# The end of the up-sampling: GpSimd makes the even columns, VectorE derives the odd ones and rectifies within its addition

## What is computed

```python
out = bilinear_resize(x, 64, 64)
out = relu(bn(conv1x1(out, conv1_w), bn1_s, bn1_b))
out = att(out, ...)             # softmax attention over N = 4096 pixels, gamma * attention + out
out = relu(bn(out, bn2_s, bn2_b))
out = bn(conv1x1(out, conv2_w), bn3_s, bn3_b)
out = bilinear_resize(out, 128, 128)
return relu(out + shortcut)     # shortcut = x
```

## Time and profile before

| | |
|---|---|
| median of 3 runs | 2825.43 us (2825.24 to 2825.67) |
| span of the profiled execution, first to last instruction | 2825.0 us |
| busy: TensorE / VectorE / ScalarE / GpSimd | 87% / 91% / 55% / 66% |
| mean granted TensorE clock | 0.960 of full speed |

### The profile page before, as it was taken

How to read it: one execution, slowest core, us unless ns; L and a number is a source line. 1 busy time by engine, 2 the same in 40 slices (tenths; PEclk the granted TensorE clock), 3 DMA queues, 4 the chain that set the end, 5 groups by cost and what they waited for, 6 DMA issues and landing times.

```text
span 2825.0 us, 53992 instructions
## 1 busy us (share of the span) xinstructions
PE 2443.9 (87%) x15912; PEld 1698.8 (60%) x15912; DVE 2561.7 (91%) x3344; ACT 1548.0 (55%) x2753; POOL 1861.1 (66%) x1536
## 2 busy tenths in 40 slices
PE   2499998898899898888889898889989999999981
PEld 1267766666566666666646666656664766666660
DVE  9978789999879999999987999999997899999989
ACT  1146655555545565555655555555654666666662
POOL 7672078888727888888833888888891255554576
PEclk8799999999999999999999999999999999999995
DMA  5321012222202222222210222222220111111123
GB/s 171 97 58 40 1 45 89 82 90 75 83 16 74 77 90 90 82 75 90 83 47 31 83 90 75 90 83 78 87 94 4 46 68 64 63 60 60 60 83 126
DMA packets 59096, 204.61 MB, mean 72 GB/s; under 512 B 8641, under 2 KB 9729, under 8 KB 58881
## 3 DMA queue, kind: packets, MB, share of 16 engines
q1 hardware_dynamic: 40448, 135.26, 14.9%
q10 hardware_dynamic: 18432, 67.12, 5.8%
HBM read 135.24 MB, written 67.11 MB: 72 GB/s over the span
## 4 chain that ended last, share of the span: by engine, by line
POOL 38%; issue 30%; PE 13%; DVE 13%; POOLq 3%; ACT 1%; DVEq 0%; DMA 0%; ACTq 0%; SPq 0%
POOL ct L334 7%; POOL cd L329 5%; POOL xin L297 5%; POOL rd L317 4%; POOL rt L322 4%; POOL y L327 3%; POOL dd L305 3%; POOL xin L301 3%; PE acc L924 2%; POOL xin L299 2%; PE acc L926 2%; PE acc L925 2%; DVE pl L597 2%; PE acc L850 2%; POOL dd L303 2%
## 5 line engine op out<-in xcount | busy, mean ns | idle before, releaser
L924 PE MATMUL acc<-vh,ph 128*128 128x257 f16 x4096 | 1160.4, 283 | 148.9 <-DVE pl L597 140.1
L926 PE MATMUL acc<-vh,pl 128*128 128x257 f16 x4096 | 1133.2, 277 | 0.0
L925 PE MATMUL acc<-vl,ph 128*128 128x256 f16 x4096 | 1131.2, 276 | 0.0
L597 DVE TENSOR_TENSOR pl<-pf,ph 128x512 f16<-128x512 f32 x1024 | 1006.0, 988 | 23.7 <-ACT pf L407 22.0
L405 ACT ACTIVATE ph<-et 128x512 f16<-128x512 f32 x1024 | 609.1, 595 | 629.9 <-PE et L802 608.8
L924 PEld LDWEIGHTS acc<-vh,ph 128*128 128x128 f16 x4096 | 403.9, 99 | 541.1 <-DVE pl L597 210.3
L407 ACT ACTIVATE pf<-et 128x512 f32<-128x512 f32 x1024 | 607.8, 594 | 29.3 <-DVE pl L597 28.6
L572 DVE TENSOR_REDUCE mx<-emx 128x1 f32<-128x512 f32 x632 | 430.7, 681 | 97.8 <-PE emx L790 95.1
L802 PE MATMUL et<-qs,ks 98*128 (+1 forms) x1024 | 497.9, 486 | 0.0
L334 POOL TENSOR_TENSOR ct<-cd,uw 128x512 f32<-128x512 f32 x248 | 374.1, 1529 | 138.9 <-DVE xres L627 126.2
L925 PEld LDWEIGHTS acc<-vl,ph 128*128 128x128 f16 x4096 | 412.0, 101 | 47.8 <-issue 20.5
(11 more groups left out here) (96 smaller groups left out, 2861.7 us busy)
## 6 DMA issues: line engine op xcount, KB each, us to landing
xres<-in_x SPq DMA_DIRECT2D x146, 512.0 KB, 4.2
out<-xres ACTq DMA_DIRECT2D x128, 512.0 KB, 2.6
xin<-in_x SPq DMA_DIRECT2D x110, 512.0 KB, 3.7
osb<-in_L_conv_conv_w SPq DMA_DIRECT2D x1, 256.0 KB, 7.5
osb<-in_L_conv_v_w SPq DMA_DIRECT2D x1, 256.0 KB, 7.6
hbuf<-in_L_conv_conv_w SPq DMA_DIRECT2D x1, 256.0 KB, 7.4
ident<-identity SPq DMA_DIRECT2D x1, 64.0 KB, 7.6
uw<-up_weights SPq DMA_DIRECT2D x1, 64.0 KB, 4.4
```

Source lines behind the costliest of these rows:

```text
L597: ops.tensor_tensor(pl[:, t % 4, :], pf[:, t % 2, :], ph[:, t % 4, :], ALU.subtract).then_inc(pl_rdy, 1)
L924: mm(acc[it][:, 0:C + 1], ph[:, tt % 4, pt], vh[:, tt, 0:C + 1], start=tt == 0, stop=False)
L925: mm(acc[it][:, 0:C], ph[:, tt % 4, pt], vl[:, tt, :], start=False, stop=False)
L926: last = mm(acc[it][:, 0:C + 1], pl[:, tt % 4, pt], vh[:, tt, 0:C + 1], start=False, stop=tt == JT - 1)
```

## The change

GpSimd multiplies the differences with the even columns' weight only (`ev`, 512 elements, contiguous), and then adds `y2`, so that `ev` holds finished even columns. The weights of the two kinds differ by a constant `STEP` per neighbour, so an odd column is the next even column minus `STEP` times the difference. VectorE does three parts in place of four:

- part 0: `edge` (the last odd column, 8 elements) takes on `y2`, and the other odd columns take on `-STEP * cd` in one `scalar_tensor_tensor`; this frees `y2` and `cd`;
- part 1: `edge` is rectified by a `tensor_scalar` maximum (8 elements), and the even columns take on `ev` and are clamped from below at 0 in one custom instruction `TENSOR_ADD_SAT`;
- part 2: the odd columns but the last take on the `ev` of the column to their right, with the same clamp.

ScalarE's rectifier goes, and the store is issued at the step where the rectifier stood. `up_v` and `up_added` count one per piece in place of two. The tables lose each piece's fourth step.

```diff
-DN, UP = 6, 5
+DN, UP = 6, 6
+STEP = (S - 1) / (H - 1)
+TOP = 3.4028234663852886e38
...
-            at_least(eng, up_v, added * 2)
+            at_least(eng, up_v, added)
...
-            at_least(eng, up_added, added * 2)
-            for parity in range(2):
-                wt = uw[:, :, parity].unsqueeze(1).broadcast_to([P, UR, S])
-                last = ops.tensor_tensor(ct_[:, :, :, parity], cd_[:, :, parity:parity + S], wt, ALU.mult)
-            last.then_inc(s, 1)
+            at_least(eng, up_added, added)
+            wt = uw[:, :, 0].unsqueeze(1).broadcast_to([P, UR, S])
+            ops.tensor_tensor(ev_, cd_[:, :, 0:S], wt, ALU.mult).then_inc(s, 1)
+            eng.wait_ge(s, base + 5)
+            ops.tensor_tensor(ev_, y2_, ev_, ALU.add).then_inc(s, 1)
...
-            def final_relu(j, i):
-
-                act.wait_ge(up_added, i * 2 + 2)
-                ops.activation(xres[:, xslot(j)], xres[:, xslot(j)], ACT.Relu).then_inc(up_relu, 1)
-
             def store(j, i, b, n, k):
                 half, row = piece_rows(n, k)
-                act.wait_ge(up_relu, i + 1)
+                act.wait_ge(up_added, i + 1)
                 act.dma_start(dram_rows(out, b, half, row, UR), xres[:, xslot(j)]).then_inc(stored[xslot(j)], 16)
...
-                rs = slice((part % 2) * (UR // 2), (part % 2 + 1) * (UR // 2))
-                xs = xres[:, xslot(j), rs, :]
+                pairs = xres[:, xslot(j)].rearrange("p r (c two) -> p r c two", two=2)
+                even, odd = pairs[:, :, :, 0], pairs[:, :, 0:S - 1, 1]
+                edge = pairs[:, :, S - 1:S, 1]
                 if part == 0:
                     dve.wait_ge(xres_ld[xslot(j)], (u - xslot(j)) * 4 + 16 * (XRES_FIRST[xslot(j)] + 1))
-                if part < 2:
-                    xs4 = xs.rearrange("p r (c two) -> p r c two", two=2)
-                    ops.tensor_tensor(xs4, xs4, y2[:, rs].unsqueeze(3).broadcast_to([P, UR // 2, S, 2]), ALU.add).then_inc(up_v, 1)
+                    ops.tensor_tensor(edge, edge, y2[:, :, S - 1:S], ALU.add)
+                    ops.scalar_tensor_tensor(odd, cd[:, :, 1:S], -STEP, odd, ALU.mult, ALU.add).then_inc(up_v, 1)
+                elif part == 1:
+                    dve.wait_ge(up_v, i + 1)
+                    ops.tensor_scalar(edge, edge, 0.0, None, ALU.max)
+                    add_relu(even, ev[:, :, 0:S])
                 else:
-                    dve.wait_ge(up_v, i * 2 + (part - 1))
-                    ops.tensor_tensor(xs, xs, ct[:, rs].rearrange("p r c two -> p r (c two)"), ALU.add).then_inc(up_added, 1)
+                    add_relu(odd, ev[:, :, 1:S]).then_inc(up_added, 1)
+
+            def add_relu(xs, up):
+
+                return ops._custom_dve(bass.dve_ops.TENSOR_ADD_SAT, out=xs, in0=xs, in1=up, s0=TOP, s1=0.0)
...
-T_ADD = ((4, 5, 6, 8), (12, 13, 14, 16), (18, 20, 21, 22), (28, 28, 29, 29))
+T_ADD = ((4, 5, 6), (12, 13, 14), (18, 20, 21), (28, 28, 29))
```

More of the change, by code:

```diff
@@ L496, in blk @@
                         bn3(g - 1, (c - 1) % 2, t_cv.index(t - 1), c == 1, c == 0)
-                    if t in t_relu and t_relu.index(t) in ups:
-                        final_relu(t_relu.index(t), ups[t_relu.index(t)][0])
-                    if t - 1 in t_relu and t_relu.index(t - 1) in ups:
-                        store(t_relu.index(t - 1), *ups[t_relu.index(t - 1)])
-                    if t == T_RELU_BEFORE and 3 in before:
-                        final_relu(3, before[3][0])
-                    if t == T_RELU_BEFORE + 1 and 3 in before:
+                    if t in t_store and t_store.index(t) in ups:
+                        store(t_store.index(t), *ups[t_store.index(t)])
+                    if t == T_STORE_BEFORE and 3 in before:
                         store(3, *before[3])
@@ L520, in _ @@
             ups = list(up_pieces(B - 1, NB - 1, NB - 1))
-            for j, u, ub, un, _, k in ups[len(T_RELU_LAST):]:
-                final_relu(j, u)
+            for j, u, ub, un, _, k in ups[len(T_STORE_LAST):]:
                 store(j, u, ub, un, k)
@@ L726, in blk @@
                     for j in ups:
-                        for part in range(4):
+                        for part in range(3):
                             if t == t_add[j][part]:
@@ L758, in _ @@
                     dve.wait_ge(late_v, done)
-                    y2_c, ct_c = buffers[2], buffers[4]
-                for part in range(4):
-                    add_part(j, u, part, LATE + i, y2_c, ct_c)
+                    made = buffers[2:]
+                for part in range(3):
+                    add_part(j, u, part, LATE + i, *made)
         @block.tensor
```

35 lines of the change are left out of this document (17 added, 18 removed).

## The result

The changed kernel takes 2841.92 us (median of 4 runs, 2840.53 to 2844.21); the kernel before, measured beside it, took 2825.34 (2825.24 to 2825.67). The ratio is 1.0054, 95% interval 1.0040 to 1.0068. The profiled spans differ by 15.0 us and the medians by 16.6: slower by some 15 us, where 82 us less had been forecast.

The account below looks back on a forecast made before the run. VectorE, partly held up by GpSimd's turns, was taken to set the time wherever pieces are added. 46 + 11 + 10 + 2.5 + 7 + 0.5 + 5 = 82 us less gave 2743.4 us, range 2705 to 2795.

Parts of the forecast that it names:

- The tail: After the last chunk: nine pieces' savings, 4.4 us, and ScalarE's last rectifier, 1.06, less a little for a wait: 5 us.
- the very last chunk: The last chunk of the last batch, with six pieces: 2.5 us less.
- the other three batch-last chunks: Last chunks of the other batches, without row maxima: 3.3 us less each, so 10 us.
- 16 middle chunks: Chunks with additions and down-sampling: 0.75 us saved on each of four pieces, 95% arriving, 2.9 a chunk, so 46 us.
- GpSimd's waits: `y2` and `ev` come free sooner, at most 3.1 us in middle chunks; GpSimd is not the bound, so nothing gained.
- 0.26 us a piece off GpSimd's turns: GpSimd's pair of line 334 becomes a contiguous multiplication and addition, taken as 0.13 us shorter each.
- 6 chunks of the last batch: Chunks without down-sampling: 3.0 us saved each, 0.6 let through because TensorE is 95% busy: 1.8, so 11 us.
- First chunks of batches: Three first chunks of batches: about 2.4 us less each, so 7 us.
- 1: Small instructions take GpSimd turns of their own: up to 120 us worse, likelier 2885; slower in all has 0.06.
- 3: Custom instruction dear: 0.57 us more each gives 2867, a third of that 2784; 2800 to 2820, shared, has 0.03.
- Rival 2: The removed addition's wait falls on its neighbour: 0.4 us a piece, 2780; 2765 to 2800, shared, has 0.25.
- Rival 4: GpSimd bounds the middle chunks at 74 us: 46 becomes 29, 2760; counted within the forecast's 0.50.

Follow-up runs that it names:

- e13: The kernel before with only the fourth part of each piece left out, a one-element maximum carrying its wait and count: 2784.3 us, ratio 0.9858.
- e4: The changed kernel with up_v, for which GpSimd's next y2 waits, counted by part 1 in place of part 0: 2824.14 us, ratio 0.9996.
- e6: The kernel before with the last piece of a middle chunk added at steps 29, 29, 30, 30 in place of 28, 28, 29, 29: 2829.43 us, ratio 1.0012.
- e8: The changed kernel with up_v given by part 1 and the last piece at steps 29, 30, 30 in place of 28, 28, 29: 2782.85 us, ratio 0.9849.
- e3: The changed kernel without the 8-element addition, and with a one-element spare maximum for the 8-element one: 2822.69 us, ratio 0.9988.
- e2: The kernel before, four parts kept, with the clamping custom instruction for the two ct additions and no ScalarE rectifier: 2826.8 us, ratio 1.0002.
- e15: e8 with GpSimd's down-sampling multiplication over 64 elements in place of 256: 2754.23 us, ratio 0.9751.

## Why the prediction was wrong

**Right: what the instructions cost VectorE.** A piece saves 0.70 us (0.75 forecast). The custom instruction costs like an addition (994 against 1017). The small ones take on the wait and spare the next. From the formula (N + 151)/0.96 ns in the Trainium skill's page "VectorE: DVE Perf Modes", section on the fixed latency of SBUF sources, I estimate 0.17 us for a lone addition of 8 elements; the lone rows show 0.16 and 0.17, the mean of 580 ns does not. No rectifier is needed for pacing. The tail gained 4.4 us (5 forecast), the very last chunk 3.7 (2.5), the other three batch-last chunks 6.7 (10), and the start of the program, up to the first group of middle chunks, 2.6 (0.5).

**Failed, the largest term: "16 middle chunks: 4 x 0.75 = 3.0 us, of which 95% arrives (VectorE's busy share)".** A busy share says how often an engine is busy, not how much of its time is on the path. The removal alone brought 0.8 us a chunk, a fifth. Most steps stand at TensorE's floor, and parts that lie there are covered. The 46 us became a loss of 9, 55 us apart. Of these, 33.5 did not come even from a removal alone, and a larger one (46 against 12.5). The other 21.5 lie between that removal and the change as it is (12.5 less against 9 more). There TensorE is idle 16.0 us longer and busy 5.4 longer (`e13` 117.4 and 1083.4, the changed kernel 133.4 and 1088.8). By the table of middle chunks the end of the chunk has little part in it (t30 3.35 against 3.20); the gaps are larger at t7, t15, t17 and t19 (0.3, 0.4, 0.3 and 0.2 us). So it is the new places of the parts and of GpSimd's instructions in the middle of a chunk, as far as the gaps tell. The later release alone does not mend them (1.4 us). The last piece placed later gives 30 us back in these chunks (1222.4 to 1192.0), by another way: the gaps around the chunk's end (t30, t0 and t1) sum to 3.97 us, against 4.66 in the changed kernel and 4.29 before.

**Failed, with a sign: "GpSimd's waits: `y2` is free after part 0 ... so nothing".** An engine off the path that is released earlier starts earlier, and here it starts in front of a `pl` and a maximum, and what stands behind them comes late. Moving the release back by one part is worth 18 us, all in the last batch. There the forecast was 11 us less and 19 more was measured; with the release as before, 413.5 stands against 414.2. The change of release is shown as cause by `e4`; that it works through the turns is read from the rows of the same instructions in both kernels. The Trainium skill's "SBUF — State Buffer", section "Who interferes with whom", says: "Issue order, not op shape, decides who blocks." It also lists `tensor_scalar` among the instructions that can take the ports shared with GpSimd. 1.45 for `pl` and 0.99 for the 8-element maximum, both begun behind a GpSimd instruction, agree. The prediction used the page's rule for the cost of instructions and not for their positions. It also took 0.26 us a piece off GpSimd's turns. Measured are 0.07 (1430 + 1554 ns for the two instructions of `ev`, 2 x 1529 for `ct`): at their shortest the two last 1.28 and 1.26 us, not the 1.03 of line 329 that they were taken for. GpSimd's busy time in the middle chunks stayed at 1019.7 us (1019.0).

**Failed: "6 chunks of the last batch ... I let 0.6 through".** As a share for a removal 0.6 is what `e13` measured (1.8 of 3.2). It was not what the change did: after it VectorE's busy time in that stretch was 382.1 against 383.7, because the turns that GpSimd now took earlier filled what the removed part had freed. With the release later again it was 373.6, and the stretch still took 413.5, no less than before: what was freed then was not ahead of a wait. The removal alone had given 10.7 us there (403.5). What in the new order of the parts takes these back, no run isolates.

**Not in the sum: the end of the chunk.** The last piece's parts stand ahead of the last `pl`s. TensorE's gap there (last batch: 1.67 before, 3.06 after) is often followed by products at the lower clock. Behind the last `pl` three parts leave a smaller gap than four, which pays in the new kernel and not in the old. So the change's saving is there to be had (47 us between `e6` and `e8`), but only with an order made for it. The kernel before was given one other order, not several, so a better one for four parts is not ruled out.

**First chunks of batches**, with the stage between: forecast 7 us less, measured 4.4 more. No run looks at them alone, and the cause is open.

**The rivals.** 1 and 3 fall by `e3` and `e2`. Rival 2, the turns stay, holds in part: the time above the lone durations, summed over `pl` and the parts, is (1118 + 1017 - 2 x 680) x 248 + (988 - 675) x 1024 = 513 us before and (1017 - 680) x 124 + (675 - 165) x 128 + (580 - 165) x 124 + (1011 - 675) x 1024 = 503 after (lone durations 675 to 680 for the large ones, 165 for the small). The removed addition's lone time went; its wait moved, 24 us of it to `pl`. Rival 4 doesn't hold: in `e15` GpSimd's shorter work arrives as shorter turns of VectorE while GpSimd's idle time grows. Of VectorE's own work two fifths arrive in the middle chunks of `e8`.

**Still open:** what decides whether the clock falls at a chunk's end, since it did not at all of them (below), and how much of TensorE's longer busy time is the clock's: no run sets it apart, and `e13` has 78.5 us at the lower clock in its middle chunks with no more busy time than before (1083.4 against 1083.7); what the remaining 1.6 us are by which `e8`'s middle chunks miss the forecast; why `e8` gives more than its two parts; and the first chunks.

## What to carry to other kernels

To price work taken from an engine, first find the steps in which the engine at its floor (here TensorE) waits for it, by its gaps per step, and ask what is removed ahead of those; the busy share of a stretch does not tell it. The gaps show where time is lost and are not yet a price: by them I allowed `e13` at most 31 us, and 42 came. Follow every semaphore that a change gives earlier: where two engines exclude each other, an earlier release moves the other one's instructions, and one that lands ahead of work on the path can cost more than the change saves there. After removing work, try the order again: here the same instructions cost 15 us with the old order and the early release, and saved 43 with another order and the release a part later.
